# Four recurrent graph blocks as one stage of 100 tiles, with a folded weight product, a pieced node update and one row in four weighted on ScalarE

## What is computed

```
for b in range(4):                                   # recurrent blocks
    agg = segment_sum((h * norm_src)[src], dst)
    g = (agg * norm_dst) @ gcn_w[b] + gcn_b[b]
    i_r, i_z, i_n = split(g @ gru_w_ih[b].T + gru_b_ih[b], 3);  h_r, h_z, h_n = split(gru_b_hh[b], 3)
    r = sigmoid(i_r + h_r);  z = sigmoid(i_z + h_z)
    h = relu((1 - z) * tanh(i_n + r * h_n))
x = layernorm(x + h)
W = silu(edge_attr @ W1 + b1) @ W2 + b2              # edge messages
agg = zeros.at[src].add(x[dst] * W)
x = layernorm(x + x + silu(agg @ W3 + b3) @ W4 + b4)  # node update
```

## Time and profile before

| | us |
|---|---|
| median of 3 runs | 6125.15 |
| the profiled execution: its time | 6125.52 |
| its span | 6123.9 |
| TensorE, VectorE, ScalarE, GpSimd busy | 4248.3, 3729.7, 1052.5, 3537.0 |
| mean granted TensorE clock | 0.851 of 2.4 GHz |

### The profile page before, as it was taken

How to read it: one execution, slowest core, us unless ns; L and a number is a source line. 1 busy time by engine, 2 the same in 40 slices (tenths; PEclk the granted TensorE clock), 3 DMA queues, 4 the chain that set the end, 5 groups by cost and what they waited for, 6 DMA issues and landing times. The chain is left out here.

```text
span 6123.9 us, 102317 instructions
## 1 busy us (share of the span) xinstructions
PE 4248.3 (69%) x26578; PEld 2961.2 (48%) x26579; DVE 3729.7 (61%) x8616; ACT 1052.5 (17%) x1881; POOL 3537.0 (58%) x3662
## 2 busy tenths in 40 slices
PE   3666667893677777774566666657777877888774
PEld 1111114662456666663455555544555555666653
DVE  8777773444799999996466666674211245555553
ACT  0111111203111111111111111112211222222221
POOL 1222223523677777771577777743666667777771
PEclk9999999996789999886577777778888889888895
DMA  4000004212444444443333333224221222222233
GB/s 202 15 13 15 13 15 181 77 27 65 122 126 117 126 119 125 119 115 122 89 82 82 76 82 82 76 70 155 63 63 54 74 72 78 77 78 78 77 78 39
DMA packets 332430, 510.95 MB, mean 83 GB/s; under 512 B 104501, under 2 KB 245855, under 8 KB 322374
## 3 DMA queue, kind: packets, MB, share of 16 engines
q0 software_dynamic: 130064, 287.19, 18.1%
q1 hardware_dynamic: 202166, 221.78, 11.2%
HBM read 406.83 MB, written 101.86 MB: 83 GB/s over the span
## 5 line engine op out<-in xcount | busy, mean ns | idle before, releaser
L1106 POOL DMA_INDIRECT e_ring<-att_rows,e_near x1760 | 1811.2, 1029 | 548.9 <-issue 472.5
L1175 PE MATMUL e_psum<-e_ring,e_whole_pick 128*128 128x264 f32 (+1 forms) x3520 | 848.6, 394 | 257.0 <-DVE e_ring L1340 249.6
L1884 POOL DMA_INDIRECT e_nodes<-x,e_edges x832 | 814.8, 979 | 265.3 <-issue 231.0
L1175 PEld LDWEIGHTS e_psum<-e_ring,e_whole_pick 128*128 128x128 f32 x3520 | 647.0, 228 | 386.1 <-issue 194.1
L1130 PE MATMUL e_px<-t_parts,e_pick 128*128 x5280 | 676.2, 269 | 82.7 <-DVE e_pick L1238 37.6
L1254 DVE TENSOR_TENSOR e_prod<-e_px,e_ring 128x512 f32<-128x512 f32 x660 | 449.8, 682 | 383.4 <-DMA e_ring<-att_rows,e_near 291.2
L285 PE MATMUL b_acc<-b_pick_key,b_pick_lo 128*128 128x416 bf16 (+1 forms) x1960 | 494.4, 340 | 171.3 <-DVE b_pick_key L256 153.0
L1801 POOL DMA_INDIRECT sorted<-rx_held,rx_index x432 | 426.8, 988 | 219.6 <-issue 208.0
L1130 PEld LDWEIGHTS e_px<-t_parts,e_pick 128*128 128x128 bf16 x5280 | 445.3, 107 | 171.9 <-issue 101.3
L1218 ACT ACTIVATE e_whole_pick<-e_pturn 128x512 f32<-128x512 bf16 x440 | 261.7, 595 | 1340.4 <-PE e_pturn L1166 1307.1
L256 DVE TENSOR_SCALAR b_pick_key<-b_lane,b_base,b_keyf 128x800 bf16<-128x800 int16 x980 | 477.3, 487 | 0.0
(11 more groups left out here) (351 smaller groups left out, 6659.9 us busy)
## 6 DMA issues: line engine op xcount, KB each, us to landing
e_relb<-place SPq DMA_DIRECT2D x56, 1024.0 KB, 5.0
e_ring<-att_rows,e_near POOLq DMA_INDIRECT x1760, 2.7
sorted<-o_fill SPq DMA_DIRECT2D x11, 2508.0 KB
e_edges<-sorted SPq DMA_DIRECT2D x209, 132.0 KB
kept<-gin_counts SPq DMA_DIRECT2D x5, 4000.0 KB, 35.5
rx_held<-in_edge_rows POOLq DMA_DIRECT2D x52, 297.0 KB
e_nodes<-x,e_edges POOLq DMA_INDIRECT x832
gru_late<-kept SPq DMA_DIRECT2D x3, 4000.0 KB, 33.0
```

Of the source, the lines that this page charges most:

```text
L1106: pool.indirect_dma_start(out=ring[:, s, r, 0:wd + HEADS], out_offset=None, in_=xrows, in_offset=bass.IndirectOffsetOnAxis(ap=near[:, s, r ...
L1175: mm = pe.matmul(psum[q % 2][:, 0:RING], whole_pick[:, q % 2, c, :], ring[:, s, q * G + c, :], start=(c == 0), stop=(c == G - 1))
L1884: pool.indirect_dma_start(out=nodes[:, q, u, :], out_offset=None, in_=source, in_offset=bass.IndirectOffsetOnAxis(ap=edges[:, q, u, RBF + ...
```

## The change

- **Recurrent blocks.** One function, `recurrent`, takes the place of four `gru_block` calls. It is written out as 100 tiles (4 blocks of 25). The sums of a tile are 25 products with the 128 by 128 block of AT stationary and the three parts side by side moving (384 columns), so the result has nodes on the partitions. ScalarE takes them out with the tile's column of `to_scale` (now 128 by 25), VectorE adds the three parts, TensorE turns them, ScalarE copies them, and one product with a folded weight gcn_w @ w_ih.T (384 columns, fp32) makes the three gates. The turn and the gate product of a tile stand among the sums of the next one. The three new bf16 parts are made tile by tile and stay in SBUF, in one of two buffers; nothing goes through DRAM between blocks. The residual is loaded once, and the LayerNorm is done once at the end.
- **Fold.** The folded weights and biases are made in `edge_order` from 12 more loads, on ScalarE, TensorE and GpSimd, and stored (1.8 MB); `recurrent` loads one block of them at a time.
- **Sends.** 404 sends stand in `recurrent`, in batches of 2 that SyncE loads into 3 buffers; 28 have moved to the second `gin_conv` (60 to 88). The copy of the slot list is gone there.
- **softmax_norm** makes the first split itself, adds the residual before the exponential is let go, and turns the degree row into a column with 25 small products.
- **Attention.** In the layer with 64 channels per head, ScalarE weights the last of the 4 rows of a pair in 4 pieces, and VectorE the other 3; TensorE waits for both. The other layer keeps its 4 rows on VectorE.
- **Node update.** x (1.6 MB) and the weights are loaded at the start of `edge_messages` after the first edge load; `x*2 + b4` is one operation there, before the last addition. The update runs in 7 parts of up to 4 tiles, with the turn of the next part ahead of the products of this one, ScalarE taking the turned tiles, and one root, one reciprocal and 25 applications at the end.

The diff, cut to its core:

```diff
+            def scale_row(k, s, q):
+                r = (q + 1) * G - 1
+                act.wait_ge(weighed, k + 1)
+                for h in range(HEADS):
+                    row = act.activation(ring[:, s, r, h * ch:(h + 1) * ch], ring[:, s, r, h * ch:(h + 1) * ch], ACT.Copy,
+                                         scale=ring[:, s, r, wd + h:wd + h + 1])
+                row.then_inc(row_scaled, 1)
...
-                rows_ = ring[:, s, q * G:(q + 1) * G, 0:wd].rearrange("p r (h c) -> p r h c", h=HEADS)
+                rows_ = ring[:, s, q * G:(q + 1) * G - BYACT, 0:wd].rearrange("p r (h c) -> p r h c", h=HEADS)
...
+                for i in range(NG + 2):
+                    if 0 <= i - 2:
+                        act.wait_ge(rest2, i - 1)
+                        act.activation(parts[:, 2, span(i - 2), :], v[:, span(i - 2), :], ACT.Copy).then_inc(lo, 1)
...
+                pe.wait_ge(clipped, 1)
+                for t in range(NT):
+                    mm = pe.matmul(psum[0][:, SC + t:SC + t + 1], row[:, t * P:(t + 1) * P], one[:, :], start=True, stop=True)
...
+                dve.tensor_tensor(x[:, :, :], x[:, :, :], v[:, :, :], ALU.add)
                 dve.drain().then_inc(step, 1)
-                dve.tensor_tensor(x[:, :, :], x[:, :, :], v[:, :, :], ALU.add)
...
+                        dve.wait_ge(lo, NG)
                         for q in range(Q):
-                            dve.tensor_scalar(to_scale[:, q * SC:(q + 1) * SC], psum[q][:, 0:SC], -1.0, 1.0, ALU.add, ALU.max)
+                            dve.tensor_scalar(row[:, q * SC:(q + 1) * SC], psum[q][0:1, 0:SC], -1.0, 1.0, ALU.add, ALU.max)
...
+                for i in range(BATCHES):
+                    if i >= 3:
+                        sp.wait_ge(sent[i % 3], 16 * SEND * (i // 3))
+                    if i == MIDDLE + 2:
+                        sp.dma_start(slot[:, :], D["slot"][:, GRU_SENDS + SENT // 2:GRU_SENDS + SENT]).then_inc(listed, 16)
+                    at = GRU_SENDS + i * SEND
+                    sp.dma_start(held[i % 3][:, :, :], D["edge_rows"][:, at:at + SEND, :]).then_inc(held_in[i % 3], 16)
...
+                for i in range(BATCHES):
+                    if i == MIDDLE:
+                        pool.wait_ge(listed, 32)
+                    pool.wait_ge(held_in[i % 3], 16 * (i // 3 + 1))
+                    for u in range(SEND):
+                        at = (i * SEND + u) % (SENT // 2)
+                        pool.indirect_dma_start(out=D["sorted"], in_=held[i % 3][:, u, :], in_offset=None,
+                                                out_offset=bass.IndirectOffsetOnAxis(ap=slot[:, at:at + 1], axis=0)
+                                                ).then_inc(sent[i % 3], 16)
...
+                    for j in range(start, stop):
+                        if b and t < 2:
+                            pe.wait_ge(lo, (b - 1) * NT + j + 1)
+                        mm = pe.matmul(ps[n % 3][:, 0:W].rearrange("p (k c) -> p k c", k=SPLIT), AT[:, j, t * P:(t + 1) * P],
+                                       parts[b % 2][:, :, j, :], start=(j == 0), stop=(j == NT - 1))
...
+                    pe.transpose(pt[n % 2][:, 0:P], red[:, :], K["identf"][:, :]).then_inc(turned, 1)
...
+                    pe.matmul(pg[n % 2][:, 0:W], turn_in[:, :], weight, start=True, stop=True).then_inc(gated, 1)
...
+                    if b and t == 0:
+                        sums(n, 0, 9)
+                        turn(n - 1)
+                        sums(n, 9, 18)
+                        gates(n - 1)
+                        sums(n, 18, 23)
+                        sums(n + 1, 0, 23)
+                        sums(n, 23, NT)
+                        sums(n + 1, 23, NT)
...
+                        sums(n, 0, 9)
+                        if n:
+                            turn(n - 1)
+                        sums(n, 9, 18)
+                        if n:
+                            gates(n - 1)
+                        sums(n, 18, NT)
...
+                    act.activation(ev[:, :], ps[n % 3][:, 0:W], ACT.Copy, scale=to_scale[:, n % NT:n % NT + 1]).then_inc(evicted, 1)
...
+                    act.activation(turn_in[:, :], pt[n % 2][:, 0:P], ACT.Copy).then_inc(turned_out, 1)
...
+                    act.activation(gate[:, 0:2 * P], gate[:, 0:2 * P], ACT.Sigmoid).then_inc(opened, 1)
...
+                    act.activation(cand, cand, ACT.Tanh).then_inc(tanned, 1)
...
+                        act.activation(parts[1 - b % 2][:, k, t, :], y[:, :], ACT.Copy).then_inc(made, 1)
...
+                            open_gates(n - 1)
+                            evict(n)
+                        tan(n - 1)
+                        part(n - 1, 0, scaled, hi)
+                        take_turn(n)
+                        part(n - 1, 1, rest, mid)
+                        part(n - 1, 2, rest2, lo)
...
+                    dve.tensor_reduce(red[:, :], ev[:, :].rearrange("p (k c) -> p c k", k=SPLIT), AX_X, ALU.add).then_inc(reduced, 1)
...
+                    dve.tensor_tensor(gate[:, :], pg[n % 2][:, 0:W], bias, ALU.add).then_inc(biased, 1)
+                    dve.wait_ge(opened, n + 1)
+                    dve.tensor_tensor(mix[:, :], reset, bhn, ALU.mult)
+                    dve.drain()
+                    dve.tensor_tensor(cand, cand, mix[:, :], ALU.add).then_inc(mixed, 1)
...
+                    dve.scalar_tensor_tensor(out=mix[:, :], in0=cand, scalar=0.0, in1=keep, op0=ALU.max, op1=ALU.mult)
+                    dve.drain()
+                    if b < LAYERS - 1:
+                        if n:
+                            dve.wait_ge(lo, n)
+                        dve.tensor_scalar(y[:, :], mix[:, :], from_scale[:, t:t + 1], None, ALU.mult).then_inc(scaled, 1)
+                        dve.wait_ge(hi, n + 1)
+                        dve.tensor_tensor(y[:, :], y[:, :], parts[1 - b % 2][:, 0, t, :], ALU.subtract).then_inc(rest, 1)
+                        dve.wait_ge(mid, n + 1)
...
+                        mixing(n - 1)
+                        state(n - 1)
+                        reduce(n)
+                    elif b and t == 1:
+                        reduce(n)
+                        mixing(n - 1)
+                        state(n - 1)
+                    else:
+                        mixing(n - 1)
+                        reduce(n)
+                        state(n - 1)
+                mixing(N - 1)
...
+GIN_SENDS = [(7 * (NT - 1), 15, 6), (7 * (NT - 1) + 90, 2, 44)]
+TABLE_SENDS = (7 * (NT - 1) + 178, 16, 2)
+GRU_SENDS = 7 * (NT - 1) + 210
+SEND = 2
+SENT = 404
...
+                    act.activation(fold[:, b, 0:P], F["pw"][b % 2][:, 0:P], ACT.Copy)
...
+                    pe.matmul(F["pw"][b % 2][:, 0:W], F["wg"][:, b, :], F["wi"][:, b, :], start=True, stop=True)
...
+                sp.dma_start(V["x"][:, :, :], source.rearrange("(t p) f -> p t f", p=P)).then_inc(kept, 16)
+                sp.dma_start(b4[:, :], D["e_b4"].partition_broadcast(P)).then_inc(kept, 16)
+                sp.dma_start(V["w3"][:, :], D["e_W3"]).then_inc(kept, 16)
...
+                dve.wait_ge(kept, 80)
+                dve.scalar_tensor_tensor(out=V["x"][:, :, :], in0=V["x"][:, :, :], scalar=2.0,
+                                         in1=b4[:, :].unsqueeze(1).broadcast_to([P, NT, P]), op0=ALU.mult, op1=ALU.add)
...
+                turn(0)
+                for i in range(N):
+                    if i + 1 < N:
+                        turn(i + 1)
+                    hide(i)
+                    if i:
+                        update(i - 1)
```

More of the change, by code:

```diff
@@ L1513, in gru_block @@
-        halves = [slice(i * HW, (i + 1) * HW) for i in range(2)]
+        second = m.sb("r_parts", [P, SPLIT * NT * P // 2])
+        parts = [whole[:, :].bitcast(BF16).rearrange("p (k t c) -> p k t c", k=SPLIT, t=NT) for whole in (first, second)]
+        out = first[:, 0:NT * P].rearrange("p (t c) -> p t c", c=P)
+        fold = m.sb("r_fold", [P, FOLD])
+        weight, bias, bhn = fold[:, 0:W], fold[:, W:2 * W], fold[:, 2 * W:FOLD]
+        ev = m.sb("r_ev", [P, W])
+        red = m.sb("r_red", [P, P])
@@ L1524, in _ @@
[L1524 to L1530 removed]
+                sp.dma_start(slot[:, :], D["slot"][:, GRU_SENDS:GRU_SENDS + SENT // 2]).then_inc(listed, 16)
@@ L1629 @@
+                dve.drain()
+                for t in range(NT):
+                    last = dve.tensor_scalar(out[:, t, :], out[:, t, :], mv[:, t, 0:1], mv[:, t, 1:2], ALU.subtract, ALU.mult)
+                    if t % GT == GT - 1:
+                        last.then_inc(done, 1)
 RBF = 64
@@ L2100, in gnn_program @@
         scratch(name, [NP, 2 * P])
-    states = []
-    for b in range(LAYERS - 1):
-        scratch(f"state{b}", [NP, P])
-        states.append(D[f"state{b}"])
+    scratch("fold", [P, LAYERS * FOLD])
     D["near"] = nc.dram_tensor("near", [P, NROW], I32, kind="Internal").ap()
```

536 lines of the change are left out of this document (327 added, 209 removed).

## The result

The changed kernel took 5850.9 us, the median of 4 runs (5845.3 to 5858.3), against 6124.3 for the kernel before; the ratio is 0.9555, 95% interval 0.9536 to 0.9573. That is 273 us less; the forecast was 249 less, 5876, with a range of 5815 to 5970. The profiled execution took 5855.07, its span is 5853.5.

What follows compares the result with a forecast made beforehand. The recurrent stage was to be bound by GpSimd's sends, 541 us over TensorE's 527. Terms -189 (recurrent), +20 (softmax_norm), -26 (attention), -59 (node update), +5 (edge_messages) sum to -249: 5876 us, range 5815 to 5970.

Steps and rivals of the forecast that it cites:

- Recurrent stage, TensorE's side: Recurrent stage: TensorE needs 5.02 us a tile, 527 us in all with boundaries, tail and barrier, at clock 1.00.
- rival E: Recurrent stage: TensorE stalls for hand-offs, one microsecond in each tile; stage 627 us, total 5962; chance 0.13.
- Recurrent stage, GpSimd's side: Recurrent stage: 404 sends at 1.31 us, 541 us with start, middle and end, set the stage; -189 us.
- Rival B: Recurrent stage: sends not slowed, 1.23 us, so TensorE's 527 bounds; total 5862, or 5829 with VectorE pacing attention; chance 0.22.
- Rival C: Recurrent stage: sends slowed as in the splitting stretch, 1.64 us each, 675 us; total 6010; chance 0.08.
- rival D: Recurrent stage: the ring of three send buffers runs dry if sends take 5 us to land; 628 us, total 5963; chance 0.10.
- The rule that was weighed: Recurrent stage: by the skill's rule, two-input VectorE operations (mix, state, subtract) slow sends; by a full effect, 1.64 us each.
- Attention: First attention layer: weighting 3 rows on VectorE shortens GpSimd's pitch by 0.03 us a gather; -26 us, bounds -5 and -59.
- Theory V: First attention layer: VectorE's load sets the pace, so taking one row off it gives -59 us.
- Node update: Node update: seven parts at 2.6 us each, one root and one store, 39.5 us for 98.5; -59 us, bounds -50 and -66.
- edge_messages: Edge messages: loading x there delays the second gather some 3 us, and a wide addition is added; +5 us.
- The fold: edge_order: 12 loads, 4 products and 1.8 MB of store beside VectorE's sorting cost nothing; 5 us of issue without that cover.

Runs made afterwards that it cites:

- gates_at_once: Against the changed kernel, each tile's turn and gate product stand right behind its own sums, not among the next tile's; 6128.5 us, 1.0015 of the kernel before.

## Why the prediction was right or wrong

**Recurrent stage, TensorE's side: right, with sizes that cancel.** Tile 5.02 forecast; 4.87 inside a block, since a turn, the gate product and 25 sums follow one another without a switching cost. That is 15 us less over 100 tiles. The boundaries cost some 14 us in all rather than 7, which makes 5.01 a tile with them, and what is left of the difference lies at the two ends of the stage, some 6 us more than the 18 forecast. Stage without sends 525.5, forecast 527. The clock was 1.00 as argued from the earlier trace rows. That the hand-offs fit between the sums (rival E, 0.13) is seen in rows with no idle time inside a block; gates_at_once shows how much hung on it.

**Recurrent stage, GpSimd's side: the sum right by luck, its terms wrong against each other.** The stage was set by the sends, as forecast: 541 forecast, 541.6 measured. But a send with its gap costs 0.983 + 0.30 = 1.28 us, not 1.31, which takes 11 us off the 404. The start and the reload in the middle came to 12.7 us (4.8 to the first send, then 4.4 of waits for loads and 3.5 for the list) rather than 8. The end cost 10.5 us where the prediction had 2.3 for the landing and 2 for the barrier; those 4.3 fit the kernel before, where 4.4 us follow the last send, and not the new stage. Had the end been known and the send not, the forecast would have been 6 us too high. Rival B, sends not slowed, had the length of a send right, 0.98 us, but not the gap, 0.30 for its 0.25, and so put the sends under TensorE's bound. Rival C, sends at 1.64, is out: the tile's 128-column operations leave them at 0.983 us. The ring all but never ran dry (rival D): loads landed in 2.1 us in the median and 4.6 at most, and GpSimd waited for one three times.

**The rule that was weighed.** The Trainium skill, "SBUF — State Buffer", section "Who interferes with whom", has VectorE instructions with two SBUF inputs contend with GpSimd instructions that read SBUF, and tensor_reduce never. The attention runs agree in kind: 1.105 us a gather with the two-input product, 1.034 with the reduction, 1.031 without either. The scans, which have two SBUF inputs, agree beside GpSimd's additions, 47.06 against 42.06. For the sends the measurement decides: by narrow operations nothing was seen (0.983 us against 0.982 before), by a wide one 0.022 us a send.

**Attention: the mechanism right, the size off.** The prediction took 0.03 us off the pitch of a gather, 0.024 of it as a quarter of the excess of 1078 ns over 982, and so -26 us. The gather fell by 0.048, and the layer by 46. The step that failed is the pricing of the shorter gather, in two places. The floor of 982 is the mean of the second layer, where 253 of 697 gathers overlap a weighting operation too and take 1.038 us; an undisturbed gather takes 0.955, the median in either layer. That makes the excess 0.124 and a quarter of it 0.031. And a quarter less weighting took more than a quarter of the excess: it went from 0.124 to 0.076, and to 0.045 with half of the weighting gone. With shorter operations fewer gathers overlap one, and each that does is held up for less: 335, 307 and 211 gathers, at 1.190, 1.117 and 1.097 us. Theory V's -59 was an end of the range; the layer does answer to VectorE's load, but at about half price (39 of 89 us), and its share fell only to 0.92, not to the 0.88 given as a sign.

**softmax_norm: right**, +22.8 for +20. **Node update: right in kind**, -66 for -59: a part takes 2.2 us rather than 2.6. The granted clock is 0.77 over the update where it was 0.50 in the earlier trace rows, and 1.00 from 5828 on, so of the parts only the first ran at the lower level. **edge_messages**: +5 forecast, -8 measured, inside the spread of that stage.

**The fold: wrong, +5 for 0.** The step that failed named VectorE's sorting as the cover and took it to cost nothing there; the 5 us that it gave for the case without cover were issue time, and that they equal the measured 5 is luck. The cover was there; GpSimd's work slowed it, 42.06 to 47.06 us of scans.

**Sum.** The spans of the two profiles differ by 270 us; the forecast was 249. The 21 are attention's 20, the node update's 7 and edge_messages' 13, less 12 for the stages ahead of attention, 3 for its second layer, 3 for softmax_norm and 1 for the recurrent stage. The rest of the way from 5876 to 5851 is the profiled execution against the median.

## What to carry to other kernels

Write out the queues of every engine before trusting "it fits": interleaving alone was worth 238 us here, and the same instructions in an unfitting order cost another 45. When work is moved under the cover of another engine, ask what both read: GpSimd's additions stretched VectorE's scans, and the weighting and the added product on VectorE stretched the gathers. A mean over a mixed lot is no floor: where fewer than half of the gathers are disturbed, their median gives the undisturbed length at once. When two queues end within some 3% of each other, as 543 and 525 us do here, first look for sends that can go where GpSimd is idle.

## What was not expected of the hardware

From the end of the new stage's last indirect send to the next stage's first issue lie 9.4 to 10.5 us, in the kernel before 4.0 to 4.4 behind the same kind of send, and 4.3 behind the last issue of a direct store. Why is open. The 25 scans of 782 columns take 47.06 us beside twelve GpSimd operations of 1.15 to 2.42 us, and 42.06 without them. Gathers of the same form take 0.955 us in the median and up to 1.8 us beside VectorE's weighting. An added VectorE reduction that leaves their length alone (1.034 us) still costs 39 us in a layer where VectorE is busy 92% and GpSimd 77% of the time.
